# Graph aggregation with residual layer norm: blocks 0 and 1 taking turns by chunk of the adjacency

## The reference

```python
def _L0_gnn_ref(x, support, weight):
    bw = jnp.sign(weight)
    ba = jnp.maximum(jnp.sign(x), 0.0)
    xw = ba @ bw.T
    out = support @ xw
    return jax.nn.relu(out)
x = _layernorm(x + _L0_gnn_ref(x, adj, L0_gnn_weight), axis=-1)   # (x - m) / sqrt(v + 1e-5)
```

## Time and profile before

| | us |
|---|---|
| median of three runs | 993.62 |
| profiled execution | 993.69 |
| its span, first to last instruction | 991.9 |
| TensorE busy | 973.0 |
| VectorE / GpSimd / ScalarE busy | 845.9 / 842.1 / 613.4 |

### The profile page before, as it was taken

One profiled execution on the slowest core, in us unless ns is written; L12 is line 12 of the kernel. 1 busy time (PEld: TensorE's weight loads), 2 busy tenths in 40 slices (PEclk: granted clock), 3 DMA queues, 4 the chain that ended last, 5 costly groups with the idle time before them and its releaser, 6 DMA issues.

```text
span 991.9 us, 12312 instructions
## 1 busy us (share of the span) xinstructions
PE 973.0 (98%) x4516; PEld 804.6 (81%) x4516; DVE 845.9 (85%) x878; ACT 613.4 (62%) x655; POOL 842.1 (85%) x361
## 2 busy tenths in 40 slices
PE   5999999999999999999999999999999999999997
PEld 3788888888888888888888888888888888888886
DVE  4768998989889898988989888898988989898894
ACT  3777675665656566565665656666565665656562
POOL 2666998998889988898898889899888998889893
PEclk9999999999999999999999999999999999999999
DMA  9999999999999999999999999999999999999971
GB/s 282 348 336 328 323 310 329 278 318 286 327 301 286 318 289 322 290 299 316 281 311 296 324 296 291 325 283 315 294 313 299 295 318 292 319 289 300 311 201 43
DMA packets 298459, 294.67 MB, mean 297 GB/s; under 512 B 9376, under 2 KB 298400, under 8 KB 298400
## 3 DMA queue, kind: packets, MB, share of 16 engines
q1 hardware_dynamic: 157792, 155.47, 57.4%
q10 hardware_dynamic: 140608, 138.43, 49.6%
HBM read 285.47 MB, written 8.39 MB: 296 GB/s over the span
## 4 chain that ended last, share of the span: by engine, by line
PE 96%; DMA 3%; DVE 0%; SPq 0%; POOL 0%; issue 0%; ACT 0%; ACTq 0%; DVEq 0%
PE ps L534 92%; DMA x_sb<-in_x_dram 1%; PE ps L603 1%; DMA raw<-in_adj_dram 1%; PE ps L517 1%; PE ps L567 1%; PE ps L507 0%; POOL lo L257 0%; SPq L180 0%; DVE stats L394 0%; DVE rows L468 0%; SPq L173 0%; PE ps L591 0%; ACT hi L277 0%; DVE mv L397 0%
## 5 line engine op out<-in xcount | busy, mean ns | idle before, releaser
L257 POOL TENSOR_TENSOR lo<-turned,hi 128x1024 fp32r<-128x1024 f32 x352 | 841.0, 2411 | 134.8 <-ACT hi L277 130.7
L534 PE MATMUL ps<-hi,xw 128*128 128x512 f32 x2032 | 794.8, 391 | 2.8 <-DVE lo L386 1.3
L534 PE MATMUL ps<-lo,xw 128*128 128x512 f32 x2032 | 791.9, 390 | 0.0
L277 ACT ACTIVATE hi<-turned 128x1024 fp32r<-128x1024 f32 x352 | 373.3, 1061 | 256.7 <-PE ps L534 173.5
L534 PEld LDWEIGHTS ps<-hi,xw 128*128 128x128 f32 x2032 | 382.0, 188 | 82.8 <-ACT xw L270 2.2
L534 PEld LDWEIGHTS ps<-lo,xw 128*128 128x128 f32 x2032 | 382.1, 188 | 78.5
L382 DVE STREAM_TRANSPOSE turned<-raw 128x1024 f32<-128x1024 f32 x352 | 426.4, 1218 | 1.1 <-DMA raw<-in_adj_dram 1.1
L386 DVE TENSOR_TENSOR lo<-ps,hi 128x1024 fp32r<-128x1024 f32 x160 | 195.3, 1220 | 107.3 <-ACT hi L277 107.3
L277 ACT ACTIVATE hi<-ps 128x1024 fp32r<-128x1024 f32 x160 | 164.1, 1026 | 92.6 <-PE ps L534 77.0
L382 DVE STREAM_TRANSPOSE ps<-raw 128x1024 f32<-128x1024 f32 x160 | 195.0, 1219 | 2.7 <-DMA raw<-in_adj_dram 2.7
L294 ACT ACTIVATE rows<-rows,shift,rstd 128x256 f32<-128x256 f32 x62 | 36.3, 587 | 0.6 <-DVE shift L405 0.6
(11 more groups left out here) (34 smaller groups left out, 76.9 us busy)
## 6 DMA issues: line engine op xcount, KB each, us to landing
raw<-in_adj_dram ACTq DMA_DIRECT2D x254, 512.0 KB, 12.0
raw<-in_adj_dram SPq DMA_DIRECT2D x254, 512.0 KB, 11.0
rows<-in_x_dram SPq DMA_DIRECT2D x16, 512.0 KB, 10.2
out_dram<-rows SPq DMA_DIRECT2D x15, 512.0 KB, 15.9
x_sb<-in_x_dram ACTq DMA_DIRECT2D x14, 256.0 KB, 12.8
x_sb<-in_x_dram SPq DMA_DIRECT2D x14, 256.0 KB, 11.1
raw<-in_adj_dram ACTq DMA_DIRECT2D x4, 256.0 KB, 8.4
raw<-in_adj_dram SPq DMA_DIRECT2D x4, 256.0 KB, 9.1
```

Of the source, the lines that this page charges most:

```text
L257: pool.tensor_tensor(lo[:, n % RING], turned[:, ordinal(n) % TP], hi[:, n % RING].bitcast(f32), ALU.subtract).then_inc(p_los_made, 1)
L277: act.activation(hi[:, n % RING], src, ACT.Copy).then_inc(his_made, 1)
L534: return pe.matmul(acc[b % 2][a], xw[:, step, a * P:(a + 1) * P], part[:, n % RING, k * MB:(k + 1) * MB], start=(step == 0 and part is hi) ...
```

## The change

**Order.** The first 16 chunks alternate between block 0 and block 1: chunk c of block 0, then chunk c of block 1. Each step of xw is so used by both blocks one after the other, and units 0 to 63 (`PAIR`) run through 16 chunks in this order. From block 2 on the order is as before. Groups g and g + 1 of xw are needed every eight units instead of every four: `NEED_AT`. `TURN_AT` and `MAKE_AT` say behind which unit TensorE does a group's turn and burst, each now alone: for odd groups the burst stands two units ahead of need (behind unit 8k) and the turn four, for even groups four and six (special values for 2 and 3, and the burst of group 1 behind unit 0). ScalarE's copy stands behind hi of unit `MAKE_AT` + 2 for odd groups and + 3 for even ones (+ 1 for group 2), its cast behind hi of `TURN_AT` + 1, VectorE's step behind the transpose of `TURN_AT` + 3 (+ 2 up to group 3).

**Chunk 0** comes in halves of its rows: 8 of 16 row tiles, all columns of a quadrant, runs of 1 KB. Its four units are halves of rows by a whole group of four tiles of columns, and TensorE works on them in 16 products of 256 columns. Units 0 and 1 are both kind V.

**Start.** W comes in two transfers, on both queues. VectorE no longer copies group 0 of xw (ScalarE does, behind hi of unit 0) nor casts group 1 (GpSimd does). Of chunk 1 one quadrant per queue is started at once, the other behind unit 0, as are the x of chunk 1 and the first part of chunk 2. `issue_at` and `x_at` have new offsets up to chunk 15.

**Ends of blocks.** The end of block 0 is worked off from unit 60 (`WORK`), that of block 1 from unit 70; rows have two buffers, and SyncE's row loads and stores have new places. The PSUM of xw moves to banks 6 and 7.

```diff
+    ORDER = [(b, c) for c in range(CH) for b in range(2)] + [(b, c) for b in range(2, NBLK) for c in range(CH)]
+    PAIR = 2 * UB
+    END = [max(n for n in range(UNITS) if ORDER[n // UPC][0] == b) + 1 for b in range(NBLK)]
+    WORK = [END[0], END[0] + 10] + END[2:]
     kinds = ["V" if n * V_UNITS % UB < V_UNITS else "P" for n in range(UB)] * NBLK
+    kinds[1] = "V"
...
+    TURN_AT, MAKE_AT, NEED_AT = {}, {1: 0}, {}
+    for g in range(GROUPS):
+        NEED_AT[g] = 2 * UPC * (g // UPG) + g % UPG * UPG
+        if g >= 2:
+            TURN_AT[g] = NEED_AT[g] - (6 if g % 2 == 0 else 4)
+            MAKE_AT[g] = NEED_AT[g] - (4 if g % 2 == 0 else 2)
+    TURN_AT.update({2: 5, 3: 7})
+    MAKE_AT.update({2: 6, 3: 8})
...
-        rows = sb("rows", [P, MT, D], f32)
+        rows = [sb(f"rows{i}", [P, MT, D], f32) for i in range(2)]
...
-        ps_xw = ps[:, 2 * BANK:4 * BANK].rearrange("p (k d) -> p k d", k=GK)
-        ps_xT = [ps[:, b * BANK:(b + 1) * BANK].bitcast(bf16).rearrange("p (k a n) -> p k a n", k=GK, a=DH)
-                 for b in (6, 7)]
+        ps_xw = ps[:, 6 * BANK:8 * BANK].rearrange("p (k d) -> p k d", k=GK)
+        ps_xT = [ps[:, (2 if g == 1 else 6) * BANK:(3 if g == 1 else 7) * BANK].bitcast(bf16)
+                 .rearrange("p (k a n) -> p k a n", k=GK, a=DH) for g in range(GROUPS)]
...
+        def rows_of(b):
+            return rows[(min(b, NBLK - 1) + 1) % 2]
...
-                              adj_v[ch // CH, ch % CH, g]).then_inc(adj_loaded[ch % SLOTS], 16)
+                              adj_v[ORDER[ch][0], ORDER[ch][1], g]).then_inc(adj_loaded[ch % SLOTS], 16)
...
-            k0, k1 = i * KG // 2, (i + 1) * KG // 2
+            t0, t1 = i * NT // 2, (i + 1) * NT // 2
             for g in quadrants:
-                eng.dma_start(raw_view(0)[g * Q:(g + 1) * Q, :, k0:k1],
-                              adj_v[0, 0, g, :, :, k0:k1]).then_inc(halves_loaded[i], 16)
+                eng.dma_start(raw_view(0)[g * Q:(g + 1) * Q, t0:t1],
+                              adj_v[0, 0, g, :, t0:t1]).then_inc(halves_loaded[i], 16)
...
-            early = 4 + 2 * half if ch < CH else max(CH + 3 - ch, 0) + half
-            return max(UPC * (ch - SLOTS + 1) + early, 0)
+            return max(UPC * (ch - SLOTS + 1) + max(5 - ch // 2, 0) + half, 0)
         def x_at(c, half):
-            return max(UPC * c - 9 + 2 * half, 0)
+            return 7 * (c - 2) + 2 + half if c > 1 else 0
+        def starts_at(n):
+            return any(n in (issue_at(ch, half), x_at(min(ch, CH - 1), half))
+                       for ch in range(1, 2 * CH) for half in range(2) if ch > 1 or n == 0)
+        def start_due(eng, n, side):
+            if n == 0:
+                start_chunk(eng, 1, side[1:2])
+            for c in range(1, CH):
+                for half in range(2):
+                    if n == x_at(c, half):
+                        start_x(eng, c + 1, side[half:half + 1])
+            for ch in range(2, 2 * CH):
+                for half in range(2):
+                    if n == issue_at(ch, half):
+                        start_chunk(eng, ch, side[half:half + 1])
...
-            sp.dma_start(w_sb, w_rows).then_inc(w_loaded, 16)
+            sp.dma_start(w_sb[:, 0], w_rows[:, 0]).then_inc(w_loaded, 16)
...
+            start_chunk(sp, 1, LOWER[0:1])
+            for n in range(PAIR):
+                if starts_at(n):
+                    sp.wait_ge(units_turned, n + 1)
+                    start_due(sp, n, LOWER)
+            load_rows(0)
+            for ch in range(2 * CH, NCHUNK):
+                sp.wait_ge(units_turned, (ch - SLOTS + 1) * UPC)
+                start_chunk(sp, ch, LOWER)
+                for b in range(NBLK):
+                    if b < NBLK - 1 and ch == -(-(WORK[b] + 26) // UPC) + SLOTS - 1:
+                        store_rows(b)
+                    if b == 1 and ch == 2 * CH + 3 or b >= 2 and ch == max(b * CH + 7, 3 * CH + 2):
+                        load_rows(b)
...
+            pool.wait_ge(x_loaded[1], G * 16)
+            pool.tensor_copy(cast_x[:, 1], x_sb[:, GK:2 * GK]).then_inc(second_cast, 1)
...
+            act.dma_start(w_sb[:, 1], w_rows[:, 1]).then_inc(w_loaded, 16)
+            start_x(act, 0, UPPER)
+            start_half(act, 0, UPPER)
             act.wait_ge(eps_set, 1)
             act.activation(warm[:], eps[:], ACT.Copy)
-            for i in range(2):
-                start_x(act, i, UPPER)
-                start_half(act, i, UPPER)
-            start_x(act, 2, UPPER)
-            start_chunk(act, 1, UPPER)
+            start_x(act, 1, UPPER)
+            start_half(act, 1, UPPER)
+            start_chunk(act, 1, UPPER[0:1])
             for n in range(UNITS):
                 make_hi(n)
-                for c in range(2, CH):
-                    for half in range(2):
-                        if n == x_at(c, half):
-                            start_x(act, c + 1, UPPER[half:half + 1])
-                for ch in range(2, NCHUNK):
+                for g in range(GROUPS):
+                    if n == (0 if g == 0 else MAKE_AT[g] + (1 if g == 2 else 2 if g % 2 else 3)):
+                        copy_xw(g)
+                    if g >= 2 and n == TURN_AT[g] + 1:
+                        cast(g)
+                start_due(act, n, UPPER)
+                for ch in range(2 * CH, NCHUNK):
                     for half in range(2):
                         if n == issue_at(ch, half):
                             start_chunk(act, ch, UPPER[half:half + 1])
-                if n < UB:
-                    g = n // UPG
-                    if n % UPG and g >= 1:
-                        copy_xw(g)
-                    if n % UPG and g + 2 < GROUPS:
-                        cast(g + 2)
-                else:
-                    ending(n // UB - 1, n % UB)
+                for b in range(NBLK - 1):
+                    ending(b, n - WORK[b])
...
+                src = raw[:, ch % SLOTS, :].rearrange("p (t k j) -> p k t j", t=NT, j=Q)
+                if ch == 0:
+                    g, t0 = u // UPG, u % UPG * NT // 2
+                    uk, src = GK, src[:, g * GK:(g + 1) * GK, t0:t0 + NT // 2]
+                else:
+                    uk, src = UK, src[:, u * UK:(u + 1) * UK]
+                dve.transpose(dst.rearrange("p (k t j) -> p k t j", k=uk, j=Q), src).then_inc(units_turned, 1)
...
-            first_cast(0)
+            dve.wait_ge(x_loaded[0], G * 16)
+            dve.tensor_copy(cast_x[:, 0], x_sb[:, 0:GK]).then_inc(first_cast, 1)
             dve.wait_ge(signs_turned, 1)
             dve.tensor_copy(sign_wT[:], ps_wT).then_inc(signs_copied, 1)
             make_step(0)
-            dve.wait_ge(xw_made, 1)
-            dve.tensor_copy(xw[:, 0:GK], ps_xw).then_inc(xw_copied, 1)
-            for n in range(UNITS):
+            turn(0)
+            make_lo(0)
+            make_step(1)
+            for n in range(1, UNITS):
                 turn(n)
-                if n == 0:
-                    first_cast(1)
-                if n and kinds[n - 1] == "V":
+                if n > 1 and kinds[n - 1] == "V":
                     make_lo(n - 1)
-                g = n // UPG
-                if n < UB and n % UPG == 0 and g % 2:
-                    make_step(g)
-                if n < UB and n % UPC == UPC - 1 and g + 1 < GROUPS:
-                    make_step(g + 1)
-                if n >= UB:
-                    ending(n // UB - 1, n % UB)
+                for g in range(2, GROUPS):
+                    if n == (TURN_AT[g] + 2 if g <= 3 else TURN_AT[g] + 3):
+                        make_step(g)
+                for b in range(NBLK - 1):
+                    ending(b, n - WORK[b])
...
+                    pe.wait_ge(xw_copied, n)
...
+                def half_product(k, a, part):
+                    step, n0 = u // UPG * GK + k, u % UPG * MB // 2
+                    return pe.matmul(acc[b % 2][a][:, n0:n0 + MB // 2], xw[:, step, a * P:(a + 1) * P],
+                                     part[:, n % RING, k * MB // 2:(k + 1) * MB // 2],
+                                     start=(n == 0 and k == 0 and part is hi), stop=False)
...
+                if n < UPC:
+                    for k in range(GK):
+                        for a in range(DH):
+                            for part in (hi, lo):
+                                last = half_product(k, a, part)
+                elif u == UB - 1:
...
-                if n < UB and n % UPG == 0:
-                    g = n // UPG
-                    if g + 1 < GROUPS:
-                        make_xw(g + 1)
-                    if g + 2 < GROUPS:
-                        turn_step(g + 2)
-                if n >= UB and n % UB == BACK_AT:
-                    turn_back(n // UB - 1)
+                for g in range(1, GROUPS):
+                    if n == MAKE_AT[g]:
+                        make_xw(g)
+                    if g >= 2 and n == TURN_AT[g]:
+                        turn_step(g)
```

(28 more changed lines are left out.)

58 lines of the change are left out of this document (17 added, 41 removed).

## The result

| | us |
|---|---|
| median before, beside it | 993.60 (993.54 to 994.08, 6 runs) |
| median after | 1001.17 (999.89 to 1002.66, 6 runs) |
| ratio after to before, 95% interval | 1.0074, 1.0064 to 1.0084 |
| profiled execution after, its span | 999.89, 998.0 |
| predicted | 1000.1, range 995.5 to 1003.0 |

The change makes the kernel slower, by 0.74%. The profiled execution grew by 6.2 us, where the prediction had 6.4; the median grew by 7.6.

A forecast was written before the change was run, and what follows sets the result against it. TensorE, holding 96% of the chain, bounds the kernel; transfers bind only the start. Start -4.4, bursts and turns +2.6, breaks +1.2, recurring waits +7.0 give +6.4 on 993.69: 1000.1 us, range 995.5 to 1003.0.

The forecast's parts named there:

- unit 0 starts: TensorE's first unit: starts at 13.4 us, 2.6 us before 15.97, held by the turn that waits for GpSimd's cast.
- unit 8 starts, against before: TensorE at unit 8: starts at 36.95 us against 41.34 before, -4.4 us.
- two more bursts and turns, more breaks: TensorE from unit 8: two more xw bursts and turns cost +2.6 us, 14 more breaks between units +1.2 us.
- recurring waits, units 11 to 60: TensorE waits for GpSimd's lo at 8k+3 because ScalarE's odd-group copy stands ahead of that hi: +7.0 us in all.
- The checkpoint: Start of unit 8, where the account compares both kernels before counting what TensorE has left to unit 63's end.
- late piece of the first stretch: TensorE before and at unit 8: waits of 0.95 (unit 3), 0.45 (unit 7), 0.8 (turn 3) and 1.2 us (unit 8).
- the cast on GpSimd: Second cast at the start, moved from VectorE: taken as 1.6 us, with x landed at 10.7.
- the earliest end of lo of unit 0: Half chunk landing at 9.2, then transpose, hi, lo and the step to TensorE: 12.9 us.
- (a): Rival: ScalarE is nowhere late, 990.6 us, chance 0.08; only the recurring waits gone, 993.1 us, chance 0.05.
- (b): Rival: earlier transfers fill the queue, issues stand on ScalarE before a hi up to 2.95 us; 1003 us, chance 0.08.

The follow-up runs named there:

- the first two experiments: Changed kernel with odd groups' copy (from group 3) behind hi of unit 8k+3: 994.92 us; the same with group 2's copy also behind hi of unit 8: 992.79 us.
- the last experiment: Kernel before with row halves and the changed kernel's start, but blocks not taking turns: 993.36 us, ratio to before 0.9996.

## Why the prediction was right

| step | forecast, us | trace of after, us |
|---|---|---|
| unit 0 starts | 13.4 | 13.15 |
| unit 8 starts, against before | 36.95, -4.4 | 36.71, -4.6 |
| two more bursts and turns, more breaks | +2.6 and +1.2 | +3.6 together |
| recurring waits, units 11 to 60 | +7.0 | +7.1, as the rest of the sum and as added up at the units |
| sum | +6.4 | +6.1 |

**The checkpoint.** Each late piece of the first stretch (units 3, 7 and 8, turn 3) was there, with the releaser named; from start to start they cost 0.6, 0.55, 0.8 and 1.1 us where the forecast had 0.95, 0.45, 0.8 and 1.2. Part of the closeness is luck: the cast on GpSimd took 1.04 us and not 1.6, while x landed later than 10.7 (the cast starts at 11.12), and in four of the seven profiles of the changed kernel and its edits x landed 0.8 to 1.3 us later still and unit 0 started between 14.00 and 14.46. The steps to the earliest end of lo of unit 0 add up to 12.8 and not 12.9; the turn held the unit, so nothing rests on it.

**Bursts and turns.** A burst pitches at 0.80 (38.62 to 39.42) and its next unit takes 1.93, where I had 0.88 and 1.90; a turn 0.43. The 0.88 was read where a turn followed, and the 0.085 for a break from the chain, while the same trace's timeline has 1.92 for such a unit; the two errors have opposite signs. Counted with the dearer unit behind them, 13 x 0.92 + 12 x 0.55 = 18.6 us stand against 15.0 in the kernel before.

**The recurring wait** was the step on which the sign hung, and the experiments test it: without the instruction in the way it goes (-6.3 us), with it one unit earlier it is larger and elsewhere (+14.0), with a shorter lo it moves one unit on, and later transfers leave it at the same places. Each wait was forecast 0.65 and cost 0.58.

**The median** came out 1.1 us above the forecast although the profiled execution was 0.2 below it. The likely cause is a fall of the clock near 36 us in some executions, which the prediction did not have; for the changed kernel itself it is not shown.

**The rivals.** (a), ScalarE nowhere late, did not happen, but the first two experiments are what it describes. It had 993.1 with the recurring waits gone and 990.6 with those of units 7 and 8 gone too; 994.92 and 992.79 were measured, 1.8 and 2.2 us more. In the second most of that lies ahead of unit 8, which started at 36.05 and not at the 34.5 that the sum gives; in the first the clock fell. (b), the queue in front of hi: one issue on ScalarE took 2.88 us from 22.56 and made unit 6 about 0.3 us late, no more; the last experiment shows the rival at nearly its full price (2.41 us of waiting, forecast 3 with a late unit 0). That transfers are ahead of need in any case, which I expected of later ones, was wrong: in the changed kernel VectorE already waits 0.25 us for chunk 2 at 30.03.

## What to carry to other kernels

In an engine's fixed order, look for an instruction that waits for another engine's newest result and stands ahead of work that this engine needs soon; add the links behind it and compare with what the waited-for engine has to do until then. One place in the order was worth 6 us or 14 us here, more than the 4.6 us by which unit 8 came sooner. And where a program moves its waits around, compare the spread of the times as well as the median.
